# Attention and mixture of experts in one kernel: the weighted sums of two score groups one behind the other, five groups of probabilities held instead of three

## The reference

```
q = (x @ Wq) -> 16 heads;  k, v = (x @ Wk), (x @ Wv) -> 4 heads, repeated 4 times
att = softmax(q @ k^T / 4 + alibi + causal)
x = layernorm(x + (att @ v) @ Wo)
logits = x @ router_w.T;  expert = argmax(logits);  xr = x * sigmoid(top logit)
gate, up = split(xr @ gate_up_proj[expert])
y = shared_expert(x) + (up * silu(gate)) @ down_proj[expert]
out = layernorm(x + y)
```

## Time and profile before

| what | value |
|---|---|
| median of 3 runs | 527.93 us (527.75 to 529.09) |
| profiled execution | 527.63 us, span 525.9 us |
| mean granted TensorE clock | 0.989 of 2.4 GHz |
| PE busy | 496.1 us, 94% of the span |
| DVE, ACT, POOL busy | 297.7, 239.1, 186.7 us |
| share of the chain that ended last | PE 79%, DVE 10%, DMA 4% |
| first weighted sum, last weighted sum | 54.55 us, 277.10 us |

### The profile page before, as it was taken

How to read it: one execution, slowest core, us unless ns; L and a number is a source line. 1 busy time by engine, 2 the same in 40 slices (tenths; PEclk the granted TensorE clock), 3 DMA queues, 4 the chain that set the end, 5 groups by cost and what they waited for, 6 DMA issues and landing times.

```text
span 525.9 us, 7405 instructions
## 1 busy us (share of the span) xinstructions
PE 496.1 (94%) x2510; PEld 244.4 (46%) x2510; DVE 297.7 (57%) x625; ACT 239.1 (45%) x480; POOL 186.7 (35%) x256
## 2 busy tenths in 40 slices
PE   5997999999999999998999999999999999999991
PEld 2443333333333333432443574646656666666650
DVE  1699889888887988892542743522123333333341
ACT  3753677667776777667674214010122222222220
POOL 4673223322131213131220600870034554555443
PEclk9998999999999999999999999999999999999996
DMA  8683635445352616173023600542031222222210
GB/s 235 123 201 103 145 118 122 138 96 186 84 194 69 210 44 196 65 242 108 20 67 96 215 0 1 163 146 71 32 88 52 70 71 71 61 70 71 62 40 30
DMA packets 36412, 54.92 MB, mean 104 GB/s; under 512 B 5191, under 2 KB 24475, under 8 KB 36268
## 3 DMA queue, kind: packets, MB, share of 16 engines
q1 hardware_dynamic: 29336, 30.96, 21.8%
q0 software_dynamic: 7040, 23.50, 14.1%
HBM read 34.76 MB, written 17.52 MB: 99 GB/s over the span
## 4 chain that ended last, share of the span: by engine, by line
PE 79%; DVE 10%; DMA 4%; POOL 2%; ACT 2%; issue 1%; SPq 1%; POOLq 0%; DVEq 0%; ACTq 0%
PE ps L822 15%; PE ps L587 11%; PE ps L562 11%; PE ps L736 9%; PE ps L576 9%; PE ps L841 8%; DVE mx L1004 6%; PE ps L749 5%; PE ps L524 3%; PE ps L833 2%; PE ps L564 2%; POOL rows L1355 1%; DMA rden<-tmp 1%; PE ps L664 1%; DMA cb<-in_cb 1%
## 5 line engine op out<-in xcount | busy, mean ns | idle before, releaser
L1004 DVE TENSOR_REDUCE mx<-ps 128x1 f32<-128x512 f32 (+4 forms) x312 | 183.1, 643 | 28.9 <-PE ps L564 22.0
L911 ACT ACTIVATE probs<-ps 128x512 f32<-128x512 f32 x288 | 152.5, 604 | 75.7 <-PE ps L576 75.6
L562 PE MATMUL ps<-qk_or_dn 127*128 127x512 bf16 (+3 forms) x384 | 116.6, 331 | 3.7 <-DVE mx L1004 2.2
L576 PE MATMUL ps<-qk_or_dn 127*128 127x512 bf16 x288 | 101.4, 380 | 1.8 <-ACT probs L911 0.8
L1322 POOL TENSOR_SCALAR_AFFINE_SELECT probs<-probs 128x512 f32<-128x512 f32 x64 | 40.5, 633 | 170.7 <-ACT probs L911 170.7
L822 PE MATMUL ps<-wgu,tmp 128*128 x184 | 82.9, 593 | 0.1
L587 PE MATMUL ps<-probs,Vs 128*32 128x512 f32 x576 | 76.7, 605 | 0.7 <-ACT probs L911 0.7
L562 PEld LDWEIGHTS ps<-qk_or_dn 127*128 127x128 bf16 x384 | 37.1, 97 | 79.3 <-DVE mx L1004 62.6
L1218 DVE TENSOR_TENSOR tmp<-tmp,ps 128x512 f32<-128x512 f32 x23 | 15.8, 688 | 65.0 <-PE ps L822 65.0
L564 PE MATMUL ps<-cb 128*128 128x128 bf16 x256 | 50.6, 222 | 0.0
L822 PEld LDWEIGHTS ps<-wgu,tmp 128*128 128x128 f32 x184 | 33.2, 190 | 33.3 <-issue 33.3
(11 more groups left out here) (134 smaller groups left out, 501.2 us busy)
## 6 DMA issues: line engine op xcount, KB each, us to landing
wgu<-in_gu POOLq DMA_DIRECT2D x8, 1024.0 KB, 5.8
qk_or_dn<-qparts SPq DMA_DIRECT2D x36, 128.0 KB
yT<-yU SPq DMA_DIRECT2D x16, 256.0 KB, 2.3
qk_or_dn<-in_dn SPq DMA_DIRECT2D x8, 512.0 KB, 6.1
tmp<-xs SPq DMA_DIRECT2D x23, 128.5 KB, 2.2
qparts<-wgu SPq DMA_DIRECT2D x6, 384.0 KB, 3.4
xs<-rows POOLq DMA_DIRECT2D x1, 2056.0 KB, 10.5
probs<-in_xT SPq DMA_DIRECT2D x4, 512.0 KB, 6.5
```

The lines of the kernel that those rows point to most:

```text
L562: mm = pe.matmul(o, q, K6[k][0:KROWS, k0:k0 + w], start=True, stop=not masked)
L576: pe.matmul(o, K6[k][0:KROWS, kb * P:(kb + 1) * P], Q6[k][0:KROWS, :, qi * P:(qi + 1) * P], start=True, stop=True).then_inc(s_st, 1)
L911: act.activation(probs[:, 4 * (s % 3) + p, :], ps[:, 4 + (4 * s + p) % SB, :], ACT.Exp, scale=SCALE).then_inc(s_exp, 1)
L1004: dve.tensor_reduce(o, ps[:, a_bank(u, t), 0:nh * w].rearrange("p (h w) -> p h w", h=nh), AX.X, ALU.max).then_inc(s_amax, 1)
```

## The change

`ORDER` now leaves the sum out of every other step and makes two of them in the next: groups 0 and 1 are summed in step 2, 2 and 3 in step 4, 4 and 5 in step 6, 6 and 7 in step 8, group 8 by itself in step 9. The numbers of S and M per step stay the same, and so does `LAST_ORDER`. So that the probabilities can wait, five groups are held instead of three: the two new places lie in the space of the gate and up weights of experts 6 and 7, and these two are loaded after the last sum, at the end of GpSimd's attention work.

```diff
-LONG, SHORT = "SMSMSMWMSM", "SMSMSMWMS"
-ORDER = (SHORT, LONG) * 4 + (SHORT,)
+HELD = 5
+LOADED = E - 2
+ORDER = ("SMSMSMSM", "SMSMSMWWMSM") * 4 + ("SMSMSMWMS",)
...
         probs = sb("probs", [P, 3 * 4, 512])
+        probs2 = wgu[:, LOADED * KC * 2 * I:E * KC * 2 * I].rearrange("p (a b) -> p a b", b=512)
+
+        def prob_at(u, s, p):
+
+            held = (u * GROUPS + s) % HELD
+            return probs[:, 4 * held + p, :] if held < 3 else probs2[:, 4 * (held - 3) + p, :]
+
...
                     mm = pe.matmul(ps[32 * j:32 * j + VP, 2 + bank, :], Vs[:, u % STEP, kb, :],
-                                   probs[:, 4 * (s % 3) + p, :], start=begins, stop=ends, skip_group_check=True)
+                                   prob_at(u, s, p), start=begins, stop=ends, skip_group_check=True)
...
+                done = 0
                 for s in range(1, GROUPS + 1):
                     at = 0
                     for c in ORDER[s - 1]:
                         if c == "M":
                             some(todo, 1)
                         elif c == "W":
-                            weigh(u, s - 1)
+                            weigh(u, done)
+                            done += 1
...
                     if p == 0:
-                        act.wait_ge(s_pv, u * GROUPS + s + 1)
-                    act.activation(probs[:, 4 * (s % 3) + p, :], ps[:, 4 + (4 * s + p) % SB, :], ACT.Exp, scale=SCALE
+                        act.wait_ge(s_pv, max(3, u * GROUPS + s + 4 - HELD))
+                    act.activation(prob_at(u, s, p), ps[:, 4 + (4 * s + p) % SB, :], ACT.Exp, scale=SCALE
                                    ).then_inc(s_exp, 1)
...
                 pool.wait_ge(s_exp, u * (4 * GROUPS) + 4 * s + 1 + SB)
-                tile = probs[:, 4 * (s % 3), :].rearrange("p (h t) -> p h t", h=HG)
+                tile = prob_at(u, s, 0).rearrange("p (h t) -> p h t", h=HG)
...
-                    if s in (3, 5) and 2 <= u < NU - 2:
+                    if s in (3, 5) and 2 <= u < 2 + LOADED // 2:
                         load_gate_up(2 * u - 4 + s // 5)
+            pool.wait_ge(s_pv, NU * GROUPS + 3)
+            for e in range(LOADED, E):
+                load_gate_up(e)
```

## The result

The changed kernel takes 532.31 us (median of 6 runs, 531.56 to 532.92); the kernel before, run beside it, 528.50. The ratio is 1.0073, 95% interval 1.006 to 1.0085: 3.2 to 4.5 us slower. The forecast was 530.7 with a range of 526.5 to 532.8. The profiled execution after took 532.92, span 531.2, mean granted clock 0.987, against 527.63 and 525.9 before.

A forecast was written before the change was run, and what follows sets the result against it. TensorE was taken to bound the attention, with VectorE and ScalarE close behind. 527.63 + 1.0 (units 0 to 5) + 0.8 (unit 6) + 1.0 (late loads) = 530.4, or 530.7 against the median; range 526.5 to 532.8.

The forecast's parts named there:

- Pairs save, waits cost: Attention units: each pair of sums saves 0.23, 0.92 per unit; uncovered waits for VectorE and ScalarE give back more.
- M26 to M29: Row-max tiles 26 to 29 of a unit: spaced 0.60, VectorE's pace, instead of 0.43; waits sum to 0.59.
- the two late scores: S(5,3) and S(1,3), score 3 of groups 5 and 1: wait 0.33 and 0.29 for ScalarE's exponentials behind copies.
- The net of a steady unit: Steady attention unit: savings and waits together make it 0.23 longer, 28.17 instead of 27.94.
- Unit 0: First attention unit: no copy of a unit before it, so it misses 0.44 of waits and is 0.2 faster.
- Unit 6: Next-to-last unit: group 2's sum no longer lies in the wait for two reciprocals; costs 0.5 to 1.06, 0.8 taken.
- The giving back by the stores: Unit 6: stores of 1/denominator, with zeros issued only 0.2 later, may win back up to 0.5.
- The late loads: After the last sum: two 1 MB loads beside the last yU store delay the last denominators; 0 to 2.3, 1.0 taken.
- The slack of 2.5: VectorE after the last reciprocal: 1.98 ahead of hidden part 1 and 0.51 ahead of the normalising.
- The lateness: Last yU store, beside the loads: between 0 and 4.8 late, 3.5 taken.
- The rival in which only the switches count: Attention units: derived waits don't come, so the kernel is faster, 525.1 or 521.5 with no waits at all; chance 0.15.
- what is given back at the turned maxima: Around the turned row maxima: the pair before gives VectorE time, so about 0.33 of the 0.13 + 0.29 waits go.

The follow-up runs named there:

- pair (6,7): Kernel before with only groups 6 and 7 summed together, in step 8; one run, 27.69 us a unit against 27.93.
- pair_23: Kernel before with only groups 2 and 3 summed together, in step 4; one run, 28.26 us a unit against 27.93.
- pair_45: Kernel before with only groups 4 and 5 summed together, in step 6; one run, 27.74 us a unit against 27.93.
- order_only: Kernel before with the new order of sums alone, three places, no late loads; 530.20 us, ratio 1.0036.
- zeros_early: Kernel before with only the zeros of the expert rows written one unit earlier; 528.19 us, ratio 0.9998.
- held_late: Changed kernel with the old order of sums, five places and late loads kept; 530.27 us, ratio 1.0035 to the kernel before.
- pairs (0,1): Kernel before with only groups 0 and 1 summed together, in step 2; one run, 28.16 us a unit against 27.93.
- late_after_rd: Changed kernel with its two late loads held back until the last reciprocal; 531.39 us, ratio 1.0048 to the kernel before.
- pairs_z: Kernel before with groups 4, 5 and 6, 7 summed in pairs and the zeros written in unit 5; 525.69 us, ratio 0.9953.

## Why the prediction came out as it did

- **Pairs save, waits cost.** Right, by its steps. Where little is uncovered, pair (6,7) shows the saving bare: 0.24, with 0.23 worked out from the earlier trace rows. The rule from the Trainium skill, "TensorEngine Tiling (Array Packing)", section Tiling Modes, that a change of the tiling mode drains the engine, agrees with that and was still no guide to the sum. M26 to M29 give 0.60 spacing, the two late scores 0.32 and 0.29 (forecast 0.33 and 0.29). The net of a steady unit was put at +0.23 and is +0.18.
- **Unit 0** was to be 0.2 faster, because no copy stands there and the waits of 0.44 behind it fall away, and was 0.13 slower. The granted clock was 1.00 in both profiles (windows from 51 to 60 us, before and then after), so these two can be compared:

```profile
51.00:60.00 9.00, 9.00 (x60) 3.50 (x59) 8.32 (x14) 6.46 (x13) 2.16 (x4) 1.00 0.73 137
```

```profile
51.00:60.00 9.00, 9.00 (x59) 3.48 (x58) 7.97 (x14) 6.30 (x13) 2.17 (x4) 1.00 0.73 138
```

The term was wrong. The copy's waits do fall away, but other waits stand in their place: ahead of the first pair the row-max tiles keep VectorE's pace of 0.60 here too, in TensorE's timeline of the changed kernel:

```profile
55.24 0.39 PE L570 MATMUL ps<-qk_or_dn 127*128 127x512 bf16 x1
...
55.84 0.39 PE L570 MATMUL ps<-qk_or_dn 127*128 127x512 bf16 x1
...
56.44 0.39 PE L570 MATMUL ps<-qk_or_dn 127*128 127x512 bf16 x1
```

The product behind this pair starts at 58.61, and the one behind the sum of group 1 before at 58.38, with the first S 0.05 later: the pair costs 0.18, nearly the 0.23 of a steady unit. In other executions unit 0 is longer because the lower granted clock reaches into it: it was 0.50 from 51 to 55 us in pair_23 and pair_45, whose unit 0 takes 30.86 and 30.32.

- **Unit 6** was put at 0.5 to 1.06, 0.8 taken. Without the fall of the clock it is 0.99 (order_only), and the mechanism is the one named: the sum of group 2 used to lie in the wait for the reciprocals, and now 0.79 of waiting stands in its place. The giving back by the stores was over-sized, 0.26 taken and 0.07 seen: with no wait for the transfer at all, zeros_early gains 0.16, since the exponentials are the next to hold the S back (0.26 in its timeline). The fall of the clock, 1.6 more in the profiled execution, was not in the sum.
- **The late loads** were put at 1.0 and cost 1.58 and 1.36 (held_late). The slack of 2.5 from the earlier trace rows was right: the reciprocal comes 4.14 later after the last sum (10.65 instead of 6.51), and the scaling 1.60. The lateness was mis-sized, 3.5 taken: I charged the store alone (3.43, only 1.1 late) and not the load of the denominators behind it (5.35, 3.0 late). What the Trainium skill's page "DMA: Bandwidth & Descriptors", section Queues, rings and completion order, says of each DMA engine going round the queues packet by packet points the same way; the order of packets shows in none of these runs.
- **The five places** were costed at nothing, and held_late's units show that. But they weren't needed, and with them the late loads: order_only costs 1.99 where the changed kernel costs 3.81.
- **The sum.** The forecast was +2.8 on the kernel before; the ratio makes it +3.8. Of the 1.0 missing, 0.58 is the loads' term, 0.19 that of unit 6 and 0.33 unit 0, less 5 x 0.05 in the steady units: 0.85. The other 0.15 stays open. The rest of the gap between 530.7 and 532.31 is that the kernel before measured 528.50 this time and 527.93 earlier. The errors of the loads, of unit 6 and of unit 0 all lie on the same side, and that the range held says little, since it is wide: from 526.5 to 532.8 it holds the kernel before as well, and the profiled execution, with the fall of the clock, is outside it at 532.92. In how many of the six runs the clock fell in unit 6 the runs don't show.

The rival in which only the switches count fell in every profile with pairs (0,1) or (2,3). Pairs (4,5) and (6,7) gain, as it has it, but not for its reason at (4,5): the wait of S(5,3) came there (0.32 in the changed kernel), and what is given back at the turned maxima outweighs it.

## What to carry to other kernels

Work that stands alone in a queue and looks expensive may be cover for a slower engine: before grouping it, ask at each place which reduction or exponential it hides, and group only where nothing comes out. A change that repeats its pattern several times should be priced place by place; here two places lost 0.55 a unit and two won 0.43, and keeping only the winners turned a loss into a gain. A load that nothing needs for a long time is still not free beside a short chain of a store and a load that the next stage waits for; each transfer of that chain can be late by itself.

## What the runs showed of the hardware that was not expected

TensorE's granted clock can fall inside the attention. In two of the fourteen profiles (the changed kernel and pair_23) it went to 1.2 GHz in unit 6, behind the waits of 0.78 or 0.79 and 1.09, and cost 1.6. In order_only and late_after_rd the same two waits stand in the same place, and no fall follows; the windows of late_after_rd show 0.91 busy of 2.00 at full clock, and full clock behind it:

```profile
234.00:236.00 2.00, 0.91 (x7) 0.27 (x10) 1.97 (x4) 0.60 (x1) 1.02 (x2) 1.00 1.01 327
236.00:238.00 2.00, 2.00 (x20) 0.63 (x13) 0.72 (x3) 0.00 (x0) 0.00 (x0) 1.00 1.00 335
```

What decides it stays open. And two stores of 32 KB took between 2.1 (pairs_z, beside one store of yU alone) and 7.6 us (pair_45, under the zeros) before SyncE could go on.
